# A two-layer graph network on one core: another order of clears, index work, loads and weight products ahead of the edge loop

## The reference

```python
h = relu(layernorm(x))
msg = (h[src] + edge_attr) @ Wm.T + bm
agg = segment_sum(msg, dst, 1250) / max(deg, 1)
update = concat(h, agg) @ Wu.T + bu
x = x + layernorm(h + gelu(update)) * gamma + beta
h = relu(layernorm(x))
rst = (1 + eps) * h + segment_sum(h[src], dst, 1250)
x = x + relu(rst @ W1 + b1) @ W2 + b2 + h
```

## Time and profile before

| | |
|---|---|
| three runs | 518.84, 520.50, 520.79; median 520.5 |
| profiled execution | 520.12, its span 518.3 |
| PE busy | 481.5 (93%), 3283 matmuls |
| DVE busy | 280.2 (54%) |
| ACT, POOL busy | 147.3, 147.1 (28% each) |
| edge groups, first and last `sums` | 29.2 to about 270 |
| mean granted clock of PE | 0.987 of 2.4 GHz |

### The profile page before, as it was taken

How to read it: one execution, slowest core, us unless ns; L and a number is a source line. 1 busy time by engine, 2 the same in 40 slices (tenths; PEclk the granted TensorE clock), 3 DMA queues, 4 the chain that set the end, 5 groups by cost and what they waited for, 6 DMA issues and landing times.

```text
span 518.3 us, 9303 instructions
## 1 busy us (share of the span) xinstructions
PE 481.5 (93%) x3283; PEld 282.5 (55%) x3283; DVE 280.2 (54%) x612; ACT 147.3 (28%) x281; POOL 147.1 (28%) x197
## 2 busy tenths in 40 slices
PE   4789999998998998699999988999989999999997
PEld 3435555544544445477774755589944447644442
DVE  6897778877877879965734867973000000001111
ACT  4325532322222226413008444750012212100000
POOL 8332334433344437600000101237993000000000
PEclk9899999999999999889999998999999999999999
DMA  8997999999999999768930110131040000011111
GB/s 299 319 344 267 361 365 365 373 366 349 369 370 356 388 369 395 299 244 323 339 104 3 42 40 20 36 122 43 1 164 0 0 0 2 0 40 42 40 40 36
DMA packets 31115, 98.97 MB, mean 191 GB/s; under 512 B 3576, under 2 KB 3576, under 8 KB 31066
## 3 DMA queue, kind: packets, MB, share of 16 engines
q1 hardware_dynamic: 30458, 97.27, 51.5%
q10 hardware_dynamic: 608, 1.05, 0.7%
HBM read 95.76 MB, written 2.56 MB: 190 GB/s over the span
## 4 chain that ended last, share of the span: by engine, by line
PE 73%; DVE 16%; issue 6%; DVEq 2%; DMA 1%; ACT 1%; POOL 0%; SPq 0%; PEldq 0%; ACTq 0%; POOLq 0%
PE ps L1309 13%; PE ps L1294 13%; PE ps L1042 7%; PE ps L1089 7%; PE ps L1241 5%; PE ps L1061 4%; PE ps L1148 4%; DVE A L685 4%; PE ps L1149 4%; PE ps L1217 4%; PE ps L1218 4%; PE ps L1070 3%; PE ps L1050 3%; DVE stats L755 1%; DVE acc L722 1%
## 5 line engine op out<-in xcount | busy, mean ns | idle before, releaser
L414 POOL TENSOR_TENSOR aggT<-turned_sums,aggT 128x88 f32 x118 | 64.0, 542 | 101.2 <-ACT turned_sums L478 87.7
L685 DVE TENSOR_TENSOR A<-ps,A 128x220 f32 x158 | 60.7, 384 | 35.8 <-PE ps L1061 25.8
L979 DVE TENSOR_TENSOR U<-ps,U 128x512 f32<-128x512 f32 (+1 forms) x10 | 6.9, 691 | 130.5 <-PE ps L1309 130.5
L1294 PE MATMUL ps<-aggT,W1s 128*128 (+1 forms) x192 | 67.4, 513 | 1.9 <-PEq L1288 1.9
L1309 PE MATMUL ps<-W2s,hid 128*128 128x512 f32 (+1 forms) x160 | 68.8, 592 | 0.0
L1042 PE MATMUL ps<-ea,oneD 128*22 128x256 f32 x944 | 62.7, 383 | 0.1
L472 ACT COPY packed_sums<-ps 128x256 f32<-128x256 f32 x59 | 22.0, 372 | 113.6 <-PE ps L1042 113.5
L1294 PEld LDWEIGHTS ps<-aggT,W1s 128*128 128x128 f32 x192 | 36.4, 190 | 32.7 <-issue 32.7
L1061 PE MATMUL ps<-oneK,oneS 128*128 128x220 bf16 x316 | 42.1, 260 | 10.7 <-DVE A L685 10.3
L1309 PEld LDWEIGHTS ps<-W2s,hid 128*128 128x128 f32 (+1 forms) x160 | 30.0, 188 | 38.2 <-issue 38.2
L1217 PE MATMUL ps<-AR,Hh 128*128 128x256 f32 (+1 forms) x160 | 44.6, 314 | 3.9 <-DVE aggT L890 3.3
(11 more groups left out here) (142 smaller groups left out, 672.9 us busy)
## 6 DMA issues: line engine op xcount, KB each, us to landing
ea<-in_edge_attr_dram SPq DMA_DIRECT2D x78, 1024.0 KB, 7.5
X<-in_x_dram SPq DMA_DIRECT2D x1, 2304.0 KB
xt<-in_x_dram SPq DMA_DIRECT2D x9, 256.0 KB, 2.8
out_dram<-U SPq DMA_DIRECT2D x9, 256.0 KB
W1s<-in_L_gnn_W_dram SPq DMA_DIRECT2D x1, 2048.0 KB, 7.8
W2s<-in_L_gnn_W_dram SPq DMA_DIRECT2D x1, 2048.0 KB, 8.6
WuN<-in_L_gnn_Wu_dram ACTq DMA_DIRECT2D x1, 1024.0 KB, 5.3
WuN<-in_L_gnn_Wu_dram SPq DMA_DIRECT2D x1, 1024.0 KB, 6.8
```

The source lines that it names most:

```text
L414: nc.gpsimd.tensor_tensor(cols, sums, cols, ALU.add).then_inc(early_step, 1)
L685: V.tensor_tensor(cols, ps[:, 4 + m % 2, half * KW:(half + 1) * KW].rearrange("p (h w) -> p h w", w=W), cols, ALU.add).then_inc(add_step, 1)
L1294: last = T.matmul(ps[:, CHUNK_BANK[k % 4], 0:cols], W1s[:, f, k * P:(k + 1) * P], aggT[:, f, bass.ds(start, cols)], start=f == 0, stop=f = ...
```

## The change

The counts A16 are cleared by ScalarE in two halves instead of by GpSimd. GpSimd's iota of pairs and the pad of x come later, and its three passes over `valid` and `big` are gone from the prologue. On VectorE the steps that lead to the keys come first (PREP_KEYS is 11 steps instead of 16), the offsets and the count of uncovered edges behind them. The turned tables are copied one at a time, with the one-hots that need them between. SP asks for edge groups 0 and 1 ahead of x; bm follows x, bu follows group 3, b1, eps and gamma come in the loop at groups 16, 20, 24. ScalarE's half of Wu is loaded in two pieces. The products 2, 3 and 4 are asides of n = 0, 1, 2. The tables for uncovered edges are made inside their branch.

```diff
-PREP_OFFS = 9
-PREP_KEYS = 16
-PREP_ALL = 18
+PREP_SPANS = 4
+PREP_KEYS = 11
+PREP_OFFS = 15
+PREP_ALL = 17
...
+    EAGER = 2
-    ASIDE = {0: ("product", FC - 1), 1: ("product", FC), 2: ("indices", 3), 3: ("indices", 4)}
+    ASIDE = {n: ("product", EAGER + n) for n in range(FC + 1 - EAGER)}
-    ASIDE_ORDER = [("product", k) for k in range(FC - 1)] + [ASIDE[n] for n in sorted(ASIDE)]
+    ASIDE_ORDER = [("product", k) for k in range(EAGER)] + [ASIDE[n] for n in sorted(ASIDE)]
+    SMALL_AT = 16
...
@@ block.sync
-            sp.wait_ge(pads_set, 3)
-            sp.dma_start(X[:, 0:NT - 1, :], ...).then_inc(x_in, 16)
-            sp.dma_start(X[0:TAIL, NT - 1, :], ...).then_inc(x_in, 16)
-            sp.dma_start(buB[:], ...).then_inc(small_in, 16)
...
             for n in range(NG):
...
+                if n == 1:
+                    sp.wait_ge(pads_set, 3)
+                    sp.dma_start(X[:, 0:NT - 1, :], ...).then_inc(x_in, 16)
+                    sp.dma_start(X[0:TAIL, NT - 1, :], ...).then_inc(x_in, 16)
+                    sp.dma_start(bmC[:], ...).then_inc(bm_in, 16)
+                if n == SLOTS - 1:
+                    sp.dma_start(buB[:], ...).then_inc(bu_in, 16)
+                if n == SMALL_AT:
+                    sp.dma_start(b1C[:], ...).then_inc(small_in, 16)
+                if n == SMALL_AT + 4:
+                    sp.dma_start(epsC[:], ...).then_inc(small_in, 16)
+                if n == SMALL_AT + 8:
+                    sp.dma_start(gammaB[:], ...).then_inc(late_in, 16)
@@ block.gpsimd
-            nc.gpsimd.memset(A16[:].bitcast(I32), 0).then_inc(counts_zero, 1)
-            pool.wait_ge(small_in, 64)
+            pool.wait_ge(bm_in, 16)
...
-            nc.gpsimd.tensor_scalar(valid[G, :], dst_f[G, :], 1.0, None, ALU.add)
-            nc.gpsimd.tensor_tensor(big[G, :], valid[G, :], big[G, :], ALU.mult)
-            nc.gpsimd.tensor_scalar(big[G, :], big[G, :], 1.0, None, ALU.subtract)
@@ block.scalar
-            act.dma_start(WuN[:, :, D:], Wu[:, D:]...).then_inc(wu2_in, 16)
+            for half in range(2):
+                cols = slice(D + half * D // 2, D + (half + 1) * D // 2)
+                act.dma_start(WuN[:, :, cols], Wu[:, cols]...).then_inc(wu2_in[half], 16)
...
+            def zero_counts(first, last):
+                words = A16[:, first:last, :].bitcast(F32)
+                nc.scalar.activation(words, iotaF[:, 0:1]...broadcast_to(...), ACT.Copy, scale=0.0).then_inc(counts_zero, 1)
+            act.wait_ge(consts, 1)
+            zero_counts(0, HB // 2)
             for n in range(2 * FC):
                 wuT(n)
-            nc.scalar.activation(aggT[:], ..., ACT.Copy, scale=0.0).then_inc(sums_zero, 1)
-            act.wait_ge(prep, PREP_OFFS)
-            act.dma_start(offrow..., offs[0:NG, :]).then_inc(offs_in, 16)
+            zero_counts(HB // 2, HB)
             product_out(0)
-            act.wait_ge(consts, 5)
-            product_out(1)
-            product_out(2)
+            act.wait_ge(prep, PREP_OFFS)
+            act.dma_start(offrow..., offs[0:NG, :]).then_inc(offs_in, 16)
+            nc.scalar.activation(aggT[:], ..., ACT.Copy, scale=0.0).then_inc(sums_zero, 1)
+            for k in range(1, EAGER):
+                product_out(k)
@@ block.vector
             step(V.tensor_copy(dst_f[G, :], dst_i[G, :]))
             step(V.tensor_reduce(m4[G, 0:2], halves(dst_f), AX.X, ALU.min))
+            step(V.tensor_tensor(halves(srel), ..., ALU.subtract))
+            step(V.tensor_scalar(hi_f[G, :].bitcast(I32), src_i[G, :], 7, None, ALU.logical_shift_right))
+            step(V.tensor_scalar(src_i[G, :], src_i[G, :], P - 1, None, ALU.bitwise_and))
+            step(V.tensor_copy(hi_f[G, :], hi_f[G, :].bitcast(I32)))
+            step(V.scalar_tensor_tensor(key[G, :], hi_f[G, :], float(W), srel[G, :], ALU.mult, ALU.add))
+            step(V.tensor_scalar(tmpf[G, :], srel[G, :], float(W), 4096.0, ALU.is_ge, ALU.mult))
+            step(V.tensor_tensor(key[G, :], key[G, :], tmpf[G, :], ALU.add))
+            step(V.tensor_copy(lo_f[G, :], src_i[G, :]))
+            dve.wait_ge(consts, 5)
             step(V.tensor_copy(offs[G, 0:2], m4[G, 0:2]))
+            assert count[0] == PREP_KEYS
             step(V.tensor_scalar(valid[G, :], dst_f[G, :], float(N), None, ALU.is_lt))
...
+            index_table(0, "srel")
             for n in range(SUM_HOTS):
                 sums_hots(n)
-            for p in range(HOTS - 1):
+            dve.wait_ge(consts, 6)
+            index_table(1, "key")
+            key_hots(0)
+            index_table(2, "lo")
+            source_hots(0)
+            for p in range(1, HOTS - 1):
                 key_hots(p)
                 source_hots(p)
             dve.wait_ge(x_in, 32)
@@ block.tensor
+                if n == 0 or n == FC // 2:
+                    pe.wait_ge(wu2_in[n // (FC // 2)], 16)
...
-            pe.wait_ge(wuT_done, 2 * FC)
             def product(k):
+                if k < 2:
+                    pe.wait_ge(wuT_done, 2 * FC - 1 + k)
...
             product(0)
             pe.wait_ge(prep, PREP_KEYS)
...
-            product(1)
-            pe.wait_ge(ct_done, 1)
-            product(2)
+            for k in range(1, EAGER):
+                product(k)
             pe.wait_ge(idxT_done, 3)
```

More of the change, by code:

```diff
@@ L284, in gnn_kernel @@
         wu1_in = sem("wu1_in")
-        wu2_in = sem("wu2_in")
+        wu2_in = [sem(f"wu2_in{half}") for half in range(2)]
         wuT_done = sem("wuT_done")
@@ L380, in _ @@
             nc.gpsimd.memset(offs[:], 0).then_inc(consts, 1)
-            nc.gpsimd.memset(A16[:].bitcast(I32), 0).then_inc(counts_zero, 1)
-            pool.wait_ge(small_in, 64)
+            nc.gpsimd.memset(X[:, NT - 1, :], 0.0).then_inc(pads_set, 1)
+            nc.gpsimd.iota(iotaP[:], [[1, 256], [0, 2]], base=0, channel_multiplier=0, allow_small_or_imprecise_dtypes=True).then_inc(consts, 1)
+            pool.wait_ge(bm_in, 16)
             nc.gpsimd.tensor_copy(bmB[:], bmC[:].rearrange("p (m a) -> p m a", a=1).broadcast_to([P, FC, P])).then_inc(bmB_done, 1)
[L386 to L393, removed]
+            pool.wait_ge(consts, 3)
             pool.wait_ge(ve_ready, 1)
@@ L630, in _, with index_table @@
             step(V.tensor_copy(offs[G, 2:3], m4[G, 2:3]))
-            step(V.tensor_scalar(hi_f[G, :].bitcast(I32), src_i[G, :], 7, None, ALU.logical_shift_right))
             assert count[0] == PREP_OFFS
[L633 to L642, removed]
+            def index_table(q, name):
                 dve.wait_ge(idxT_mm, q + 1)
@@ L820, in _ @@
                         dve.wait_ge(early_step, n * 2)
+                        V.tensor_scalar(valid[G, :], dst_f[G, :], 1.0, None, ALU.add).then_inc(gen_prep, 1)
+                        V.memset(idxT["hit"][:], 0.0).then_inc(gen_out, 1)
+                        dve.wait_ge(gen_prep, 1)
+                        V.tensor_tensor(big[G, :], valid[G, :], big[G, :], ALU.mult).then_inc(gen_prep, 1)
+                        dve.wait_ge(gen_prep, 2)
+                        V.tensor_scalar(big[G, :], big[G, :], 1.0, None, ALU.subtract).then_inc(gen_prep, 1)
+                        for q, name in enumerate(("hi", "dE")):
+                            dve.wait_ge(gen_turned, q + 1)
+                            turned_table = ps[:, 6 + q, 0:SUB * GP].rearrange("p (j g) -> p j g", j=SUB)[:, :, 0:NG]
+                            V.tensor_copy(idxT[name][:, :, 0:NG], turned_table).then_inc(gen_out, 1)
+                        dve.wait_ge(gen_out, 3)
                         V.tensor_copy(idxT["lo"][:, :, 0:NG], pairT["lo"][:, 0:NG].rearrange("p g h j -> p (h j) g")).then_inc(lo_ready, 1)
@@ L1008, in product, with transpose_indices @@
                 last.then_inc(ct_mm, 1)
[L1010 removed]
+            def transpose_indices(mine, to, ready):
                 for j in range(SUB):
@@ L1013, in transpose_indices @@
                     last = T.transpose(ps[:, to, j * GP:j * GP + NG], mine[0:NG, cols], ident[0:NG, 0:NG])
-                last.then_inc(idxT_mm, 1)
+                last.then_inc(ready, 1)
             pe.wait_ge(wm_in, 16)
@@ L1169, in _ @@
                             bank_free(what)
+                        pe.wait_ge(gen_prep, 3)
+                        for q, mine in enumerate((hi_f, big)):
+                            transpose_indices(mine, 6 + q, gen_turned)
+                        pe.wait_ge(gen_out, 3)
                         T.sem_inc(gen_mm, 1)
```

58 lines of the change are left out of this document (27 added, 31 removed).

## The result

Before: median 520.55 (518.4 to 523.17, 20 runs). Changed: median 523.5 (521.58 to 530.67, 20 runs). The ratio is 1.0051, 95% interval 1.0034 to 1.0067: slower by 1.8 to 3.5 us, where a loss of 1.0 us was forecast. The forecast had drawn the line to "slower" at 523.1: the result lies just over that line, inside the stated range of 518.0 to 524.2. The profiled execution of the changed kernel took 526.07 (span 524.3).

A forecast was written before the change was run, and what follows sets the result against it. VectorE was taken to bound the prologue up to 37.69, TensorE the loop's first groups. -3.0 (x) + 2.6 (products) + 1.4 (clock) = +1.0, so 521.1, with 0.4 to the median 521.5; range 518.0 to 524.2.

The forecast's parts named there:

- Counts cleared by ScalarE, keys first: VectorE's index work: conversion at 0.42, 3.4 gained; keys at 13.4 instead of 19.2; transposes at 16.6, behind product(0).
- Edges ahead of x: SP's loads: x lands at 24.7 behind two edge groups, bn_stats start at 24.8, 3.0 gained up to the first add.
- Two products in the loop: TensorE, counts(2) to sums(4): product 3 now behind the wait, +3.5, less 0.9 of transposes: +2.6.
- The clock: TensorE after six idle us before counts(2): 1.4 lost on products 3 and 4, bounds 0 and 2.8.
- From sums(4) on the shift is carried to the end unchanged: Loop from sums(4): both engines follow each other as before, so nothing is added to or taken from the shift.
- The credit of 0.9 for the index transposes: TensorE in the loop: the hi and big transposes are left out, 0.44 each, so -0.9.
- A: First groups of the loop: VectorE's adds set the pace, products and clock don't show; faster, 517.5; chance 0.14.
- C: TensorE after its idle time before counts(2): no loss of clock, sum -0.4, 520.1; chance 0.12.
- B: SP queue: x comes late behind two edge groups, at 26.5 with doubled clock loss +4.1, 524.6; slower; chance 0.16.
- its doubled loss of clock: TensorE behind the wait before counts(2): the clock low for twice as long, costing 2.8.
- their upper ends (2.3, 1.4 and 1.5): Forecast's upper bounds: x landing later +2.3, clock +1.4, small loads in the loop (b1C, eps, gamma) +1.5.
- 1 KB runs: Load of ScalarE's half of Wu, ahead of Wm: 0.4 more for 1.05 MB, bounds 0 and 2.7.

The follow-up runs named there:

- e4: The changed kernel with GpSimd clearing A16 again, behind its iota of pairs; median 524.32, ratio to the kernel before 1.0053.
- e3: The changed kernel with four extra matmuls in TensorE's idle time before counts(2); median 522.69, ratio to the kernel before 1.0030.
- e5: The changed kernel with x loaded ahead of the first edge groups again; median 522.62, ratio to the kernel before 1.0033.
- e1: The kernel before with products 2, 3 and 4 moved into the loop, index transposes at groups 3 and 8; median 529.69, ratio 1.0151.
- e2: The changed kernel with product 2 back ahead of the loop; median 519.37, ratio to the kernel before 0.9945.
- e8: The changed kernel with six extra matmuls in TensorE's idle time before counts(2); median 522.47, ratio to the kernel before 1.0019.
- e10: The kernel before with its bias product done ahead of counts(2) instead of behind it; median 518.87, ratio 0.9954.
- e7: The changed kernel with products 3 and 4 both ahead of counts(2); median 515.61, ratio to the kernel before 0.9894.
- e9: The changed kernel with products 3 and 4 ahead of counts(2) and x loaded ahead of the edges; median 515.45, ratio to the kernel before 0.9884.
- e6: The changed kernel with product 3 ahead of counts(2) instead of behind it; median 519.37, ratio to the kernel before 0.9972.

## Why the prediction was right or wrong

A small loss was forecast and a small loss came, by the forecast's mechanism in the main, but the size was short: +1.0 forecast, +3.25 at group 7, +2.95 in the medians, which is just over the forecast's line to "slower", a side that it had given 0.17. That the range held the result is in part luck, as one step failed and two terms were short. By its steps:

- *Counts cleared by ScalarE, keys first.* Right: 0.42 at L627, keys at 13.1 (13.4), and the index work hidden behind `product(0)`; e4 shows that it is worth nothing. The transposes came at 18.30 instead of 16.6, since `product(0)` began 0.6 later than forecast and took 4.78 (3.70 before) with its first matmuls at half pace. In e3 they came at 16.68. It cost nothing, as the one-hots were ready just before x.
- *Edges ahead of x.* Right: 25.15 against 24.8, and 1.02 come back when x goes first (e5). The gain at the first add was 2.54 instead of 3.0: 0.46 short.
- *Two products in the loop.* +2.6 between `counts(2)` and `sums(4)`: right. The stretch went from 8.73 to 13.55, 4.8 more, of which 2.3 are the clock (1.97 on product 3, 0.3 on `counts(2)`) and 2.5 are left. e1 and e2 show the term from both sides.
- *The clock.* The right cause, and for this trace mis-sized: 1.4 came from the one row at hand, 2.3 was measured twice (trace, and e8 by its difference), inside the bounds of 0 and 2.8. Taken the same way, e2, e3, e4 and e5 lost 1.4, 1.7, 1.6 and 1.4, and e1 lost 2.2. The idle times before were 2.60, 3.47, 6.07, 4.91 and 4.75: the length of the idle time doesn't order the losses, so 1.4 was no bad figure for a loss that varies between 1.4 and 2.3.
- *"From sums(4) on the shift is carried to the end unchanged."* This step failed. `sums(7)` came 8.22 after `sums(4)`, before 7.25: +0.97. VectorE had been starved until 48.59 by product 4, and then its adds, one-hots and the copy of the bias product ran with hardly a pause to 56.0 and held TensorE up (0.27 and 0.66). The credit of 0.9 for the index transposes was worth nothing by group 7: it seems that they had filled just this time. For it, the stretch from `sums(4)` to `sums(7)` took 7.25 and 7.18 in the two runs that still have both transposes ahead of it (before, e10), and 7.84 to 8.24 in the changed kernel and the eight built on it. Two of the eight are e7 and e9 (7.85 and 7.84), in which no product stands in the loop behind group 1's sums to starve VectorE. No run put the transposes back into the changed kernel, so this part is argued. From group 7 on the shift was carried unchanged to group 58.

Of the rivals, A (the backlog is swallowed) is excluded by VectorE's waits of 4.72 and 3.68 for TensorE. C (no loss of clock) fell by the trace (0.51 in 32.9 to 39.8). B named x as the cause, which landed 0.4 late and no more; its doubled loss of clock is what partly came. The sum by what was measured: -2.54 + 2.5 + 2.3 + 0.97 = 3.2. One reading of my own bounds was wrong too: I said that the range held them all, but their upper ends (2.3, 1.4 and 1.5) together give 526.7, and the range ended at 524.2.

Not settled: how the clock's behaviour varies from one execution to the next. The changed kernel's runs spread over 6.3 us even without the 530.67 where before's spread over 4.8, and the traces from 200 on show the clock low for different stretches with the same work; no run was made that separates this.

## What to carry to other kernels

When engines run through a fixed order, price a moved step by which wait it stands before and which it stands behind: the same product cost 3.5 us behind `counts(2)` and nothing ahead of it (e6 against the changed kernel). Work that has slack anywhere (the blocks of CT that these products make are first read at 279, behind the edge loop) belongs into the longest wait of its own engine, where it also keeps that engine's clock up. And when a wait is shortened on one engine, look at once at what its partner was doing in that time; here the earlier first add and the idle TensorE were two halves of a gain of 5 us, of which the change made one.

## What the runs showed of the hardware that I had not expected

After 2.37 and 2.60 us of idle TensorE the clock fell (0.54 in 35.5 to 39 of e6; the bias product at 4.71 in e2), after 1.76 (before) and 0.57 (e8) it didn't. This makes no limit near 2 us, as other idle times in the same traces show. After 1.83 in e1 and 1.98 in e10, up to 19.25, it fell (product 1 took 5.34 in e1). And where TensorE waits 1.46 to 1.77 for Wu, up to about 10.4, it fell in e6, e7 and e8 (0.50 in 12 to 15) and not in e3, e5 and e9 (1.00), after 1.77, 1.53 and 1.64 against 1.75, 1.55 and 1.60. `product(0)` of e6:

```profile
13.53 4.54 PE L1029 MATMUL ps<-Wu2T,WmN 128*128 128x512 f32 x8
```

The same product took 3.67 in e3. In the changed kernel's own trace it took 4.78 after 1.46, though that trace's rows have 1.00 there. Behind the 3.47 idle us of e3 the clock fell not at the end of the idle time but a product later: the first instruction behind the wait ran at the high level, the next at the low one. A gain at the wait itself is therefore no sign that the clock's loss was avoided.

Cutting ScalarE's half of Wu into 1 KB runs cost nothing that shows: SP's two loads beside and behind it, its half of Wu and Wm, landed 6.8 and 9.0 after their issue in both kernels (9.0 for Wm in the earlier trace rows), where I had allowed for 0.4.
